# First matrices of a chain of per-sample layers: transfers and matmul operands addressed from registers in place of indirect gathers and one-hot picks

## The chip, the cores and the metric

One core of a Trainium2 chip runs the kernel. The metric is the device time of one execution in microseconds, as the median of several runs. The core has TensorE (PE, matmuls), VectorE (DVE), ScalarE (ACT), GpSimd (POOL) and SyncE (SP, which only issues transfers). SBUF and PSUM have 128 partitions; PSUM has eight banks of 128 x 512 fp32.

## The reference, cut

```python
# x (64, 64, 512) fp32; subject (64,) in 1..198, adapter (64,) in 0..7; C = 64 channels
x = x + einsum('bct,bcd->bdt', x, L0[subject])              # L0: 200 matrices 64 x 64
x = x + einsum('bct,bcd->bdt', x, L1[adapter])              # L1: 8 matrices
x = x + einsum('bct,bcd->bdt', x, L2[adapter]) + bias[adapter][:, :, None]
# then a gated MLP over the last axis, 512 -> 2048 -> 512, each matrix with a
# rank-16 correction chosen by adapter:
gate = x @ Wg + (x @ Ag[adapter]) @ Bg[adapter];  up = likewise with Wu, Au, Bu
h = silu(gate) * up
x = x + h @ Wd + (h @ Ad[adapter]) @ Bd[adapter]
```

With identities added, the first three layers of a sample are one 64 x 64 matrix, (I + L0[subject]) (I + L1[adapter]) (I + L2[adapter]), and a bias.

## The kernel before, in words

The 64 samples stand as 32 pairs (two samples of 64 channels fill 128 partitions), and the pairs are worked in four quarters of eight, each quarter in two halves t of four (TP = 4). For each quarter the MLP runs over 16 hidden blocks, called units; products are fp32 split in a high and a low fp32r part, and a Strassen-like scheme turns eight products of halves into seven. The matrices for quarters 1 to 3 are made while the units of the quarter before run. The opening, the code before the loop over units, makes those of quarter 0, with nothing to run beside. The change touches this opening alone. All order is written by hand: each engine has its own program and waits on semaphores.

The opening before, by engine:

- **SyncE** loads the subjects (`ints`), L2 (`w2_four`) and L1 (`w1_four`), waits for both, loads the first half of x (`load_x(0, 0)`), then after six picks the first weights (`load_weights(0)`), after the first gathers the second half of x, then b rows (`load_b(0)`); it stores `es_four` in `e_table`, waits for all four `w_done`, loads the weights of unit 1 and `bd_rows`, and goes on to `store_ad`, `store_b`.
- **VectorE** makes the row numbers of the gathers (`gather_numbers`), adds the identity to L2 (`e2_four`), compares the adapters of the quarter's samples with 0 to 7 (`eq_first`), adds to the product of L1 and I + L2 what makes it (I + L1)(I + L2) and keeps it in `es_four`, with zeros on both sides. It then makes for each of the eight pairs a one-hot pick matrix (`picks`, line 1334), widens what was picked (`picked`, 1342), and adds after the combining (`o_combine`, 1387). Numbers for later gathers follow (`block_rows`, `row_numbers`, `block_numbers`), `tables`, the low parts of the turned tokens (1454), `selectors` (1404), and from 1465 on the sums of tokens and their low parts (`o_low`, 1395), then `select` (1572, 1576).
- **GpSimd** issues eight indirect gathers of L0 rows (`ea_four`, line 766), then that of `ad_rows` (`gather_ad(0, 0)`), the low part of the b rows (`b_low(0)`, 803) and the gathers of `b_got`.
- **ScalarE** loads the adapters and the bias, makes the high parts of the first weights (`wg_hi`), adds the bias to each layer's result (974), copies the turned tokens (943), and between the halves makes the high part of the b rows (`b_high(0)`).
- **TensorE** runs 14 warm-up matmuls of 128 x 128 x 128 (`WARM_UP`, 1758), L1 times I + L2 (1913), the bias by pair (1917), 4 more warm-ups, the picks (1925: four matmuls of 64 columns a pair, one for each two adapters), the combining with the gathered L0 rows (1934: one matmul of 128 columns a pair), the layers (1943: one of 512 columns a pair) and the turns (transposes, 1762: four a pair), half 0 ahead of half 1, with only the combining of half 1 put before the turns of half 0. Then `first_product` begins at once with line 1735.

Each fp32 matmul stands in the trace as two passes, so that 16 picks' matmuls are 32 entries.

## Time and profile before

| | us |
|---|---|
| median of 3 runs | 1239.54 |
| lowest and highest of them | 1239.38, 1240.88 |
| the profiled execution, its own time | 1237.63 |
| its span, first to last instruction | 1235.8 |
| TensorE busy in the span | 1227.7 |
| first big product begins (line 1735) | 28.78 |

Times in the rows are counted from the span's start. A group in a timeline is a run of like instructions on one engine: its start, the time from its first start to its last end, and in brackets how long the engine had been idle before and what released it. A pass's duration overlaps its neighbours', so that the spacing of starts is the rate. A row such as "SPq" or "ACTq" is the issue of a transfer, and "to landing" is from the issue to the last byte.

### The profile page before, as it was taken

How to read it: one execution, taken by the hardware profiler on the slowest of the kernel's cores; microseconds unless marked ns; L12 is line 12 of the kernel's file. 1: busy time of each engine (PE TensorE's matmuls, PEld its weight loads, DVE VectorE, ACT ScalarE, POOL GpSimd, SP SyncE). 2: the span in 40 equal slices, each digit the busy share in tenths (PEclk: the TensorE clock that was granted, in tenths of full speed). 3: DMA queues.
4: the chain of work that ended last, by engine and by line, in shares of the span. 5: the costliest groups of instructions: out<-in, count | busy, mean ns of one | idle time of the engine just before them, and what ended most of it. 6: DMA issues, size and time to landing. Idle time of an engine off the chain costs nothing.

```text
span 1235.8 us, 18085 instructions
## 1 busy us (share of the span) xinstructions
PE 1227.7 (99%) x6190; PEld 1029.7 (83%) x6190; DVE 957.1 (77%) x1540; ACT 558.1 (45%) x1003; POOL 710.7 (58%) x598
## 2 busy tenths in 40 slices
PE   9999999999999999999999999999999999999998
PEld 8888888888888888888888888888888888888886
DVE  7887777887688777788678778777868877677775
ACT  4744445444544344454344444444534443444333
POOL 4676655558736556546864556555675554444453
PEclk9999999999999999999999999999999999999999
DMA  6866455556865455557496544546659442322323
GB/s 213 295 214 220 126 153 186 162 163 185 289 223 162 124 158 144 164 162 213 142 332 191 178 128 143 166 137 187 198 180 314 160 120 80 93 84 86 113 89 107
DMA packets 141690, 209.60 MB, mean 170 GB/s; under 512 B 44192, under 2 KB 88480, under 8 KB 141600
## 3 DMA queue, kind: packets, MB, share of 16 engines
q1 hardware_dynamic: 117696, 135.45, 34.8%
q0 software_dynamic: 23040, 71.85, 19.0%
q8 instruction: 51, 0.84, 0.3%
q10 hardware_dynamic: 864, 1.15, 0.3%
q14 instruction: 39, 0.32, 0.1%
HBM read 164.36 MB, written 44.04 MB: 169 GB/s over the span
## 4 chain that ended last, share of the span: by engine, by line
PE 97%; DVE 2%; issue 0%; ACT 0%; POOL 0%; DVEq 0%; POOLq 0%
PE px L1735 29%; PE pd L1735 28%; PE py L1735 14%; PE pz L1735 7%; PE pz L1752 3%; PE pv L1781 2%; PE pv L1779 2%; PE pd L2074 2%; PE py L1752 2%; PE px L1752 2%; PE pd L1762 1%; PE px L1886 1%; PE py L1886 1%; PE pd L1871 1%; PE px L1758 1%; PE pd L1904 0%
## 5 line engine op out<-in xcount | busy, mean ns | idle before, releaser
L803 POOL TENSOR_TENSOR h_lo<-g,h_hi 128x512 fp32r<-128x512 f32 x127 | 182.4, 1437 | 298.0 <-ACT h_hi L943 297.2
L766 POOL DMA_INDIRECT b_got<-b_table,idx_b x192 | 198.5, 1034 | 59.9 <-issue 49.9
L1735 PE MATMUL px<-xo_hi,wg_hi 128*128 128x512 f32 x516 | 207.2, 402 | 1.3 <-DVE wg_lo L1382 0.9
L1513 DVE TENSOR_TENSOR acc<-pd,acc 128x512 f32<-128x512 f32 x248 | 164.3, 684 | 51.6 <-PE pd L1735 51.6
L1382 DVE TENSOR_TENSOR wg_lo<-w_raw,wg_hi 128x512 fp32r<-128x512 f32 (+1 forms) x256 | 182.8, 720 | 26.5 <-ACT wg_hi L943 26.4
L1735 PE MATMUL px<-xo_hi,wg_lo 128*128 128x512 f32 x516 | 202.5, 392 | 0.0
L1735 PE MATMUL px<-xo_lo,wg_hi 128*128 128x512 f32 x516 | 201.0, 389 | 0.0
L943 ACT ACTIVATE wg_hi<-w_raw 128x512 fp32r<-128x512 f32 (+1 forms) x260 | 146.0, 570 | 121.1 <-PE py L1752 74.6
L1735 PE MATMUL pd<-wd_hi,h_hi 128*128 128x512 f32 x504 | 199.7, 396 | 0.0
L1735 PE MATMUL pd<-wd_lo,h_hi 128*128 128x512 f32 x504 | 197.9, 393 | 0.0
L1735 PE MATMUL pd<-wd_hi,h_lo 128*128 128x512 f32 x504 | 196.6, 390 | 0.0
L943 ACT ACTIVATE h_hi<-g 128x512 fp32r<-128x512 f32 x128 | 80.9, 632 | 195.0 <-DVE g L1607 76.1
L1735 PEld LDWEIGHTS px<-xo_hi,wg_lo 128*128 128x128 f32 x516 | 96.8, 188 | 22.1
L1735 PEld LDWEIGHTS px<-xo_hi,wg_hi 128*128 128x128 f32 x516 | 96.9, 188 | 19.1 <-issue 2.3
L1735 PEld LDWEIGHTS pd<-wd_hi,h_lo 128*128 128x128 f32 x504 | 94.6, 188 | 21.8
L1735 PE MATMUL py<-xo_hi,wg_hi 128*128 128x512 f32 x260 | 111.6, 429 | 0.0
L1735 PEld LDWEIGHTS px<-xo_lo,wg_hi 128*128 128x128 f32 x516 | 97.5, 189 | 15.6
L1735 PEld LDWEIGHTS pd<-wd_hi,h_hi 128*128 128x128 f32 x504 | 94.6, 188 | 13.9
L1735 PEld LDWEIGHTS pd<-wd_lo,h_hi 128*128 128x128 f32 x504 | 94.8, 188 | 12.8
L1617 DVE TENSOR_TENSOR g<-g,up 128x512 f32<-128x512 f32 x64 | 100.4, 1569 | 3.6 <-ACT g L1181 2.7
L943 ACT ACTIVATE g<-px 128x512 f32<-128x512 f32 x64 | 38.2, 598 | 141.2 <-PE px L1735 141.2
L1735 PE MATMUL py<-xo_hi,wg_lo 128*128 128x512 f32 x260 | 101.8, 391 | 0.0
(331 smaller groups left out, 2439.6 us busy)
## 6 DMA issues: line engine op xcount, KB each, us to landing
w_raw<-w_gu SPq DMA_DIRECT2D x65, 512.0 KB, 4.8
wd_raw<-w_dn SPq DMA_DIRECT2D x64, 256.0 KB, 3.5
xo_hi<-xops SPq DMA_DIRECT2D x21, 512.0 KB, 6.0
xo_lo<-xops SPq DMA_DIRECT2D x21, 512.0 KB, 7.3
acc<-x SPq DMA_DIRECT2D x8, 1024.0 KB, 6.8
ad_raw<-ad_table SPq DMA_DIRECT2D x16, 512.0 KB, 4.3
ad_table<-ad_rows_kept SPq DMA_DIRECT2D x12, 512.0 KB, 6.5
xops<-st_hi SPq DMA_DIRECT2D x24, 256.0 KB, 2.8
```

The source lines that it names most:

```text
L766: gp.indirect_dma_start(out=dst, out_offset=None, in_=rows_of, in_offset=bass.IndirectOffsetOnAxis(ap=rows.bitcast(U32), axis=0)).then_inc ...
L803: return gp.tensor_tensor(dst, src_raw, src_hi, ALU.subtract)
L943: return act.activation(dst, src, ACT.Copy)
L1382: dve.tensor_tensor(wg_lo[:, lo:hi, :], weights_of(n, g), wg_hi[:, lo:hi, :], ALU.subtract).then_inc(w_done[g], 1)
L1513: ins = dve.tensor_tensor(dst, pd[j][:, :], dst, ALU.add)
L1617: dve.tensor_tensor(g1[:, :], g1[:, :], up1[:, :], ALU.mult).then_inc(h_done[1], 1)
L1735: ins = pe.matmul(psum, w_parts[wi], x_parts[xi], start=(start and i == 0), stop=(stop and i == 2), skip_group_check=more)
L1752: ins = pe.matmul(psum[:, tokens], b_got[:, CHUNKS * t + c, first:first + P], u[:, m, t, cols], start=(start and c == 0), stop=True, skip_ ...
L1779: pe.matmul(pv[:, tok], ad[:, half, 2 * t + a, :, :].rearrange("p g n -> p (g n)"), hs[0][:, tok], start=(half == 0 and a == 0), stop=True ...
L1781: ins = pe.matmul(pv[0:HC, tok], ad[:, half, 2 * t + a, 0, :], hs[1][:, tok], start=False, stop=True, skip_group_check=True)
L1886: ins = pe.matmul(ua_bank(q, t, 0)[:, a * HALF:(a + 1) * HALF], w_parts[wi][:, cols], (xo_hi, xo_lo)[xi][:, k, tok], start=(cp == c == a = ...
L2074: pe.matmul(pd[0][:, :], f_one[:, :], acc[:, (q + 1) % 2, PAIR_ORDER[i], :], start=True, stop=True).then_inc(layer_mm, 1)
```

## The change

- SyncE and ScalarE each read the 16 subjects of quarter 0 from DRAM into registers, and TensorE the 16 adapters (`first_values`). The row transfers of L0 are plain transfers of 64 rows for one sample, with the address from a register (`first_rows`): samples of half s = 0 on SyncE's queue, s = 1 on ScalarE's, four for each half t and queue, 16 in all.
- L1 and L2 are laid out by adapter on 64 partitions (`w1_all`, `w2_all`) and loaded on ScalarE's queue. Their product takes eight matmuls of 64 columns in place of four; `es` holds for each adapter zeros, the matrix, zeros.
- Picks, widening and the addition after the combining go. The identity is added to the L0 rows before (`first_sum`, VectorE, in place), and the combining is one matmul of 64 columns a sample whose right operand is `es_cols` at a column from a register. ScalarE copies the result out of PSUM (`f_four`), two pairs a copy.
- Warm-up matmuls 11 and 4, not 14 and 4. Layers and turns are interleaved on TensorE: layers 0, 1, 2, turn 0 of half 0, layer 3, turn 1 and so on; ScalarE's bias additions and copies follow that order.
- The high part of the first weights and of the first b rows move from ScalarE to GpSimd, where the eight gathers were.
- SyncE's waits in the opening go in part: weights of unit 0 and both halves of x are issued behind row transfers without one; the weights of unit 1 come before the store of `e_table`. VectorE makes index numbers, tables and selectors directly after the second sum of rows, and waits for the store of `e_table` before the first sums of tokens, since `es` now lies where S1 is written.

```diff
-WARM_UP = (14, 4)
+WARM_UP = (11, 4)
...
+        es_cols = flat(acc[0:C, 1, 2:5, :])
+        es = by_adapter(es_cols)
+        w1_all = by_adapter(up1[0:C, :])
+        w2_all = by_adapter(g0[0:C, :])
+        e2 = by_adapter(g1[0:C, :])
+        ea = [flat(acc[0:C, 1, i:i + 2, :]).rearrange("p (s n) -> p s n", s=2 * TP) for i in (0, 6)]
+        f_four = [four(up0[:, :]), four(vacc[:, 0, :])]
...
+        of_banks = ((pz, pd[2]), (px, pv))
+
+        def first_rows(engine, t, s, subjects):
+
+            of_half = w0_rows[s * SUBJECTS * C:(s + 1) * SUBJECTS * C].rearrange("(u c) n -> u c n", c=C)
+            for j in range(TP):
+                rows = of_half[bass.ds(subjects[2 * (TP * t + j) + s], 1)].rearrange("u c n -> (u c) n")
+                engine.dma_start(ea[t][:, 2 * j + s, :], rows).then_inc(oe_in[t], 16)
...
-            sp.wait_ge(ints_in, 2 * 16)
-            sp.wait_ge(e0_in, 2 * 16)
+            sp.dma_start(ints[:, 1, :], adapter.partition_broadcast(P)).then_inc(ints_in, 16)
+            subjects = first_values(mybir.EngineType.SP, subject, SUBJECTS)
+            first_rows(sp, 0, 0, subjects)
             load_x(0, 0)
-            sp.wait_ge(pick_made, TP + 2)
+            first_rows(sp, 1, 0, subjects)
             load_weights(0)
-            sp.wait_ge(oe_in[0], TP * 16)
             load_x(0, 1)
             sp.wait_ge(x_in[0][1], 16)
             load_b(0)
+            load_weights(1)
             sp.wait_ge(oe_add, 1)
...
-            gp.wait_ge(idx_done, 1)
-            for t in range(2):
-                for j in range(TP):
-                    gather_rows(ea_four[t][:, j, :], w0_rows, idx_first[:, TP * t + j:TP * t + j + 1], oe_in[t])
+            gp.wait_ge(raw_in[0], 16)
+            for g in range(4):
+                gp.tensor_copy(wg_hi[:, 2 * g, :], w_raw[:, 0, g, :]).then_inc(w_hi_done[g], 1)
             gp.wait_ge(idx_a_done, 1)
             gather_ad(0, 0)
+            gp.wait_ge(*piece_in(0))
+            gp.tensor_copy(part(st_hi[:, piece(0)[0], :]), st_lo[:, piece(0)[0], :]).then_inc(b_hi_done, 1)
             b_low(0)
...
-            act.dma_start(ints[:, 1, :], adapter.partition_broadcast(P)).then_inc(ints_in, 16)
+            act.dma_start(w2_all, w2_rows.rearrange("p (a n) -> p a n", a=ADAPTERS)).then_inc(e0_in, 16)
+            act.dma_start(w1_all, w1_cols.rearrange("p (a n) -> p a n", a=ADAPTERS)).then_inc(e0_in, 16)
+            subjects = first_values(mybir.EngineType.Activation, subject, SUBJECTS)
+            first_rows(act, 0, 1, subjects)
             act.dma_start(bias_src, bias_pairs).then_inc(bias_in, 16)
+            first_rows(act, 1, 1, subjects)
+            act.dma_start(ints[:, 0, :], subject.partition_broadcast(P)).then_inc(subjects_in, 16)
...
+            for t in range(2):
+                for i in range(2):
+                    act.wait_ge(of_mm, 2 * t + i + 1)
+                    copy(f_four[t][:, 2 * i:2 * i + 2, :], four(of_banks[t][i][:, :])[:, 0:2, :]).then_inc(of_kept, 1)
...
+            for p in range(3):
+                o_bias(p)
+            for j in range(TP):
+                o_a1_high(j)
+                o_bias(j + 3)
+            o_bias(QP - 1)
+            for j in range(TP):
+                act.wait_ge(o_turn, TP + j + 1)
+                copy(acc[:, 1, :, j * P:(j + 1) * P].rearrange("p (k c) n -> p k c n", c=2)[:, 0:4:3],
+                     turn_banks[j][:, :].rearrange("p (k c n) -> p k c n", k=2, c=2)).then_inc(o_a2_kept, 1)
...
+            def first_sum(t):
+
+                dve.wait_ge(oe_in[t], 2 * TP * 16)
+                own_part = ea[t].rearrange("p (j s) (h n) -> p j (s h) n", s=2, h=2)[:, :, 0:4:3, :]
+                dve.tensor_tensor(own_part, own_part, ident[0:C, 0:C].unsqueeze(1).unsqueeze(1).to_broadcast([C, TP, 2, C]),
+                                  ALU.add).then_inc(ea_done, 1)
...
+            first_sum(0)
             dve.wait_ge(e2_done, 1)
             dve.wait_ge(oe_mm, 1)
-            dve.tensor_tensor(es_four[:, :, C:2 * C], four(pv[:, 0:TP * C]), e2_four, ALU.add).then_inc(oe_add, 1)
+            dve.tensor_tensor(es[:, :, C:2 * C], by_adapter(pv[0:C, :]), e2, ALU.add).then_inc(oe_add, 1)
+            first_sum(1)
+            row_numbers()
+            block_numbers()
+            tables()
+            gather_numbers()
+            selectors(0, 0)
...
             sums(1)
+            dve.wait_ge(e_out, 2 * 16)
...
+            adapters = first_values(mybir.EngineType.PE, adapter, ADAPTERS)
             pe.wait_ge(consts, 5)
             warm_up(WARM_UP[0])
             pe.wait_ge(e0_in, 2 * 16)
             pe.wait_ge(e2_done, 1)
-            for j in range(TP):
-                ins = pe.matmul(pv[:, j * C:(j + 1) * C], w1_four[:, j, :], e2_four[:, j, :], start=True, stop=True)
+            for i in range(ADAPTERS):
+                ins = pe.matmul(pv[0:C, i * C:(i + 1) * C], w1_all[:, i, :], e2[:, i, :], start=True, stop=True)
             ins.then_inc(oe_mm, 1)
...
             def o_combine(t):
-                pe.wait_ge(oe_in[t], TP * 16)
-                pe.wait_ge(eb_done, t + 1)
+                pe.wait_ge(ea_done, t + 1)
                 for j in range(TP):
+                    for s in range(2):
+                        first = j % 2 * P + s * C
+                        column = adapters[2 * (TP * t + j) + s] * (3 * C) + C
+                        ins = pe.matmul(of_banks[t][j // 2][:, first:first + C], ea[t][:, 2 * j + s, :],
+                                        es_cols[:, bass.ds(column, C)], start=True, stop=True)
+                    if j % 2:
+                        ins.then_inc(of_mm, 1)
...
-            picked(range(TP + 2))
             o_combine(0)
-            picked(range(TP + 2, QP))
-            o_layers(0)
+            o_combine(1)
             pe.wait_ge(bias_done, 1)
-            o_combine(1)
+            o_layer(0)
+            o_layer(1)
             for j in range(TP):
-                pe.wait_ge(o_layer_a, j + 1)
-                turn(0, 0, j, pd[j]).then_inc(o_turn, 1)
-            o_layers(1)
+                o_layer(j + 2)
+                o_turned(0, j)
+            o_layer(6)
+            o_turned(1, 0)
+            o_layer(7)
+            for j in range(1, TP):
+                o_turned(1, j)
```

## Rows read from the trace of the kernel before

**Rows 1.** The page: span, busy time by engine, chain by engine.
```profile
span 1235.8 us, 18085 instructions
PE 1227.7 (99%) x6190; PEld 1029.7 (83%) x6190; DVE 957.1 (77%) x1540; ACT 558.1 (45%) x1003; POOL 710.7 (58%) x598
...
PE 97%; DVE 2%; issue 0%; ACT 0%; POOL 0%; DVEq 0%; POOLq 0%
```

**Rows 2.** TensorE's waits after the warm-up, whole span: waiting line, releaser, us in total, times, longest.
```profile
PE px L1735 <- DVE wg_lo L1382: 0.9, 1, 0.9
PE px L1735 <- DVE up L1560: 0.4, 1, 0.4
```

**Rows 3.** Timeline of TensorE, opening: start, length, engine, line, operation, tiles, count.
```profile
1.94 5.78 PE L1758 MATMUL px<-ident 128*128 128x128 f32 x28 [1.94 <-POOL ident L810]
7.55 1.00 PE L1913 MATMUL pv<-acc 128*128 128x64 f32 x8
...
8.59 1.14 PE L1758 MATMUL px<-ident 128*128 128x128 f32 x8
9.56 1.90 PE L1925 MATMUL pz<-vacc,g 128*128 128x64 f32 x16
...
14.87 1.11 PE L1934 MATMUL pv<-acc 128*128 128x128 f32 x8
...
17.55 3.65 PE L1943 MATMUL pd<-acc 128*128 128x512 f32 x8
...
28.78 0.48 PE L1735 MATMUL px<-xo_hi,wg_hi 128*128 128x512 f32 x1
...
48.00 0.48 PE L1752 MATMUL pz<-u,b_got 128*128 128x192 f32 x3
```

**Rows 4.** Timeline of VectorE, opening.
```profile
16.09 0.69 DVE L1387 TENSOR_TENSOR acc<-pv,acc 128x512 f32<-128x512 f32 x1 [0.85 <-PE pv L1934]
...
18.64 0.14 DVE L1262 TENSOR_SCALAR f_one<-f_one 128x1 int32<-128x1 int32 x1
18.70 0.16 DVE L1263 TENSOR_SCALAR f_one<-ea_one 128x16 int32<-128x16 int32 x1
...
30.23 1.29 DVE L1465 TENSOR_TENSOR acc<-acc 128x512 f32<-128x512 f32 x2
...
47.04 0.54 DVE L1576 TENSOR_TENSOR u<-pd,u_mask 128x384 fp32r<-128x384 f32 x1
```

**Rows 5.** Timeline of ScalarE, opening: the first issue, a copy of turned tokens.
```profile
0.75 0.41 ACTq L977 DMA_DIRECT2D eb_one<-adapter  x1
...
28.85 0.61 ACT L943 ACTIVATE acc<-pv 128x512 f32<-128x512 f32 x1
```

**Rows 6.** Timeline of GpSimd, opening: one of eight gathers, b_low, a gather of b_got.
```profile
16.41 0.94 POOL L766 DMA_INDIRECT acc<-w_rows,st_lo  x1 [0.30 <-issue]
...
25.65 2.38 POOL L803 TENSOR_TENSOR st_lo<-st_lo,st_hi 128x1024 fp32r<-128x1024 f32 x1 [2.04 <-ACT st_hi L943]
...
40.11 1.24 POOL L766 DMA_INDIRECT b_got<-b_table,idx_b  x1 [0.16 <-issue]
```

**Rows 7.** Timeline of SyncE's queue, opening: the halves of x.
```profile
6.66 0.38 SPq L570 DMA_DIRECT2D acc<-x  x1
...
14.59 0.38 SPq L570 DMA_DIRECT2D acc<-x  x1
```

**Rows 8.** Transfers issued up to 45 us: kind, count, KB each, median us to landing.
```profile
acc<-x SPq DMA_DIRECT2D x2, 1024.0 KB, 5.3
...
acc<-w_pairs SPq DMA_DIRECT2D x1, 256.0 KB, 4.9
...
acc<-w_rows,st_lo POOLq DMA_INDIRECT x8, 3.7
b_got<-b_table,idx_b POOLq DMA_INDIRECT x5, 5.6
...
eb_one<-subject SPq DMA_DIRECT2D x1, 32.0 KB, 3.7
```

173 lines of the change are left out of this document (46 added, 127 removed).

## The prediction

> **What bounds the kernel now.** I read the page first: TensorE is busy 1227.7 us of a span of 1235.8 us, and the chain of work that ended last is TensorE for 97% [rows 1]. The list of TensorE's waits over the whole span has, after the 1.94 us before the first warm-up matmul [rows 3], one entry of 0.9 us and one of 0.4 us [rows 2]. So TensorE's stream is packed from 1.94 us on, and a change to the opening is worth exactly the time by which it brings forward the first big product (called T below, 28.78 us now), if nothing behind it becomes late. The timeline of TensorE says what fills the time to T [rows 3]: 28 warm-up passes from 1.94, the eight passes that multiply L1 with L2 at 7.55, eight more warm-up passes, and then from 9.56 to 17.55 the one-hot picks (64 passes of 64 columns in five rows, of which one stands) and the first combining (8 passes, 14.87). From 17.55 to T run layers, combining for the second half and turns. (Each fp32 matmul is two passes.)
>
> The other engines are close behind. VectorE works without a gap from the weight parts near 16.7 to 48 us; its first token sums start at 30.23, 1.45 after T, and its selection ends at 47.58 [rows 4], where TensorE's product with b_got, which needs it, starts at 48.00 [rows 3]: 0.4 us of slack. Whoever brings T forward must bring this VectorE chain forward by as much.
>
> **Removed on TensorE.** 9.56 to 17.55 is 7.99 us; less about 1.0 for the combining in it, the picks are 7.0 us, 0.11 us a pass [rows 3]. All go. VectorE loses eight picks, two widenings and two additions, all of the shape that takes 0.69, some 8 us [rows 4]; the eight indirect gathers leave GpSimd.
>
> **Added on TensorE.** The combining is now one matmul a sample: 16 matmuls, 32 passes of 64 columns. At the picks' rate that is 32 x 0.11 = 3.5 us, against 2 x 0.95 for the old 2 x 8 passes: +1.6. The L1-L2 product has 16 passes instead of 8, with stationary operands half as wide; between no change and 8 x 0.11 = 0.9. I take 0.5, and it lies where TensorE otherwise warms. Three warm-up matmuls fewer free 6 x 0.2 = 1.2 us there. Layers and turns are the same instructions in another order: 28.78 - 17.55 less 0.9 for the second combining (8 passes like those at 14.87) = 10.3 us [rows 3]. If only TensorE's work counted, T would move by 7.0 - 1.6 = 5.4 us, and by some tenths more for the warm-ups. But now operands decide, so I follow those.
>
> **Reading registers.** SyncE, ScalarE and TensorE each read 16 integers from DRAM into registers first. No row shows such a read. The nearest rows are one issue of a transfer, 0.41 [rows 5], and the landing of the smallest one, the 32 KB of subjects, 3.7 [rows 8]. I take 1.1 us, near the low end, because 64 bytes move and no transfer is built; the ends stay for the range. On TensorE it lies beside the 1.94 us that it waits for the identity [rows 3], so up to 1.2 us of it costs nothing.
>
> The Trainium skill, page "Runtime: NRT & Kernel Launch", section "Instruction fetch mechanics", puts a register load at about 200 ns a register even in bulk. By that estimate 16 registers are 3.2 us, the row addresses are known 2.1 us later, and the gain below shrinks to 2.6 us. No run here shows it yet.
>
> **Row transfers with addresses from registers.** An issue is 0.38 to 0.41 us [rows 5, 7]. To it come some two or three register operations; the nearest row is the step between two tiny independent VectorE instructions, 0.06 us (18.64 to 18.70) [rows 4], so 0.5 to 0.6 in all; I take 0.6, and for the range 0.4 to 1.0. ScalarE issues the L2 and L1 matrices (0.9), reads (1.1), issues 4 rows (2.4), the bias (0.4) and 4 rows (2.4): from 0.75 it ends at 8.0. SyncE issues the adapters (0.4), reads, 4 rows, x's first half (0.4), 4 rows: it ends at 7.45, with x's first half issued at 5.0, where it was 6.66 [rows 7]. A transfer of this size lands 3.7 after its issue as an indirect gather, with 0.94 us of GpSimd's own work in it [rows 6, 8]; behind a megabyte of x I take 3.3. The first eight rows are then there at 4.55 + 3.3 = about 8.0, the second eight at 7.4 + 3.3 = 10.7.
>
> **The chain to T.** L1, issued second at 1.2, lands in 4.9 [rows 8], at 6.1; 0.68 of VectorE for the sum with the identity gives 6.8, TensorE's product 8.2. First sum of rows, 0.69 [rows 4], ends at 8.7, the addition into es at 9.4. The bias lands near 5.6 + 4.0 = 9.6, and TensorE waits for it ahead of four warm-ups (1.0) [rows 3]: 10.7 at worst, and the eight matmuls of the first combining (1.8) run to about 12.0 with some overlap of my allowances. The second needs the second rows: 10.7 + 0.69 = 11.4. So rows and TensorE meet near 11.7, the second combining ends at 13.5, and layers and turns run on to 23.8. TensorE's reading of its operand address from a register costs between nothing (its sequencer is ahead of the array) and 16 x 3 x 0.06 = 2.9 us; nearest is nothing, since the picks also ran at 0.11 a pass and a matmul here fills the array for 0.22; I take 0. The new order has ScalarE copy the first turn of the second half after all eight bias additions, so T waits for that copy: 0.61 [rows 5], of which half lies beside the last turn: +0.3. T = 24.1, gain 28.8 - 24.1 = 4.7 us.
>
> **Does the rest follow?** VectorE: the second half of the first sums could start when the fourth copy is done, T + 0.9, and end at T + 1.6, where it ended at 31.52 = T + 2.7 [rows 4]; its slack grows by 1.1. Ahead of that it has, from 11.4 on, the numbers for indices, tables and selectors (6 us), weight parts (1.4), and low parts of the first turns as they come: done before T. The e_table store, which VectorE now awaits before the sums, is issued some 8 us ahead of them and lands like x within 5.3 us [rows 8]; cover 2.7 us, and if gone it delays VectorE by what is missing. GpSimd takes two jobs from ScalarE: the four weight copies (bounded by 1.2 and, as its subtraction, 2.38 for 1024 columns) and the first b copy (same bounds) [rows 6]. Queued behind them are gather_ad, b_low and the b_got gathers. The indices come at about 13, not 22, and the weights by 12.5, so even at 2.4 + 2.4 this queue is still some 4 us earlier than now; the gather at 40.11 lands 5.6 later [rows 6, 8], 2.3 before the product at 48.00 needs it [rows 3], and its predecessor, the b copy on ScalarE, moves with T. The second half of x is issued near 8.8 rather than 14.59 and lands within 5.3 [rows 8], before layer 4 at 17.9. What is late next is VectorE again, no worse than now. I count nothing for it.
>
> **Sum.** The profiled execution took 1237.63 us, its span 1235.8 [rows 1] and 1.8 around it; 1237.6 - 4.7 = 1232.9. The median of the runs shown lies 1.9 above it, 1239.54, so 1239.54 - 4.7 = 1234.8.
>
> **Rivals.**
> A, register work is dear: reading costs 3.3 us, near the 3.7 of a small landing [rows 8], not 1.1, or TensorE's operand addresses cost their 2.9. Either moves T to 26.3 to 27.0, gain 1.8 to 2.5: 1237.4. For it: no row excludes it. Against: the gap in TensorE's work while it waits for rows hides half of the second.
> B, the other sign: the registers are read one after another with a round trip each. Beyond 1.1 + 4.7 = 5.8 us for 16, or 0.36 each, T is later than now. At 0.5 us each it is 8.0: T = 31.0, 2.2 us slower, 1241.8. For it: a small transfer's round trip is 3.7 us [rows 8]. Against: one read of a few words has no transfer's descriptors.
> C, TensorE's clock. The profile grants 1.00 (2.4 GHz) in its clock row throughout, yet the first 28 passes take 0.21 us each and the later eight 0.14 at most [rows 3], so some slowness stands at the start. New holes, ahead of the rows, could bring it back for a few us: at double length for 3 us of work T moves by 3, 1237.9. The Trainium skill, page "TensorE: Matmul & The Clock Gate", section "HAM oscillation — how this bites in real kernels", says that holes in the stream return TensorE to 1.2 GHz; that would be this case. My holes are 1 to 2 us, with work between.
> D, something later is late: the gain at T is given back in units 1 to 3, by b_got or VectorE. Time 1239.5. Against: the slacks above.
> E, rows land in 2.3 us rather than 3.3 and issues cost 0.45, so that the second rows are there by 8.4 and TensorE's own stream decides: 6.8 + 1.4 (product) + 0.2 (bias) + 1.0 (warm-ups) + 3.5 + 10.3 = 23.2, or 22.7 if the product takes 0.9. Gain 5.6 to 6.1: 1233.4 to 1233.9. Nothing in these rows allows more. Against: the bias too would have to land by 8.
>
> **How the numbers follow.** Forecast 0.55 (1234.0 to 1236.0 by itself), A 0.15, B 0.06, C 0.06, D 0.06, E 0.12. A measurement of this kernel can tell about 0.2%, 2.5 us. Faster by more: forecast, E, a third of A and C: 0.55 + 0.12 + 0.07 = 0.74, and a little of the forecast's neighbours, 0.76. Slower by more: half of B and a little for unnamed causes, 0.06. Same 0.18. The range reaches over E, with half a microsecond for the spread of the runs, and most of A and C: 1232.9 to 1238.0.
>
> **What would show it.** Right: TensorE's first big product near 24.1; L1758's second group followed by 32 passes in 3.5 us or with one gap of 1 to 2 us in it, released by VectorE's sum of rows; layers and turns in 10.3 to 10.6 us; TensorE's waits after T unchanged at about 1.3 us. A: the first row transfers on SyncE issue later than 2.5 us, or the 32 passes are spaced by more than 0.11. B: they issue after 7. C: layer passes longer than 0.65 us. D: new entries in the list of TensorE's waits after T. The prediction is wrong if T moves and the time does not, or if T moves by less than 3 us.

## The result and the profile after

| | before | after |
|---|---|---|
| median, us | 1239.57 | 1245.18 |
| lowest, highest of 5 runs | 1239.38, 1240.88 | 1245.07, 1245.43 |
| profiled execution, own time | 1237.63 | 1245.23 |
| its span | 1235.8 | 1243.3 |
| first big product begins (T) | 28.78 | 35.63 |
| span less T | 1207.0 | 1207.7 |

The change makes the kernel slower by 5.6 us: ratio 1.0043, interval 1.0032 to 1.0054. The forecast was 1234.8, at most 1238.0. The last row of the table says where to look. Behind T the two executions are the same within 0.7 us, so the loss lies in the opening. The profiled execution of before took 1.7 us less than the lowest of its five runs, so the two profiles differ by 7.6 us where the medians differ by 5.6; what follows splits T of the profiles. Two later executions, one of x7_interleave and one of x11_best, took about 1735 us at a mean clock of 0.65, and the medians below count them while the ratios leave them out.

The page of after, span, busy time, and shares of the chain by engine, against rows 1:

```profile
span 1243.3 us, 18046 instructions
PE 1229.8 (99%) x6144; PEld 1029.0 (83%) x6144; DVE 950.9 (76%) x1523; ACT 557.5 (45%) x1002; POOL 705.2 (57%) x595
...
PE 96%; DVE 2%; issue 1%; ACTq 0%; DMA 0%; ACT 0%; DVEq 0%
```

TensorE runs 46 passes fewer than before and is nevertheless busy 2.1 us longer. Some of its passes must have become slower. Its waits in after, whole span (waiting line, releaser, us in total, times, longest), against rows 2:

```profile
PE px L1743 <- issue: 4.7, 1, 4.7
PE py L1903 <- DMA vacc<-bias_pairs: 2.1, 1, 2.1
PE px L1720 <- DVE wg_lo L1379: 0.9, 1, 0.9
PE px L1720 <- DVE up L1545: 0.7, 1, 0.7
PE px L1720 <- ACT up L944: 0.3, 1, 0.3
```

Two are new: the start at 4.7 instead of 1.94, and 2.1 us for the bias. The last three, behind T, sum to 1.9 us, where before had 1.3. The timeline of TensorE in after shows the order, against rows 3:

```profile
4.69 5.04 PE L1743 MATMUL px<-ident 128*128 128x128 f32 x22 [4.69 <-issue]
9.65 1.69 PE L1899 MATMUL pv<-g,up 64*64 64x64 f32 x16
13.43 0.41 PE L1903 MATMUL py<-st_lo,vacc 128*128 128x32 f32 x2 [2.09 <-DMA vacc<-bias_pairs]
...
15.09 1.97 PE L1913 MATMUL pz<-acc 64*128 x8
...
22.11 5.49 PE L1922 MATMUL pd<-acc,up 128*128 128x512 f32 x6
...
35.63 0.47 PE L1720 MATMUL px<-xo_hi,wg_hi 128*128 128x512 f32 x1
```

The 32 combining passes (line 1913) run from 15.09 to 22.1: 7.0 us, 0.22 a pass, where the picks took 0.11. The first three layers (line 1922, six passes) take 5.49, or 0.91 a pass; half of that is what a pass took before (3.65 for eight). From 28.1 on the passes have their old length. So from 14 to 28 us TensorE ran at half speed, and the windows of after say so too (window, its length, PE's busy time and passes, granted clock, DMA share, GB/s):

```profile
12.00:14.00 2.00, 0.57 (x5) 1.00 1.20 283
14.00:16.00 2.00, 2.00 (x12) 0.58 0.84 265
...
26.00:28.00 2.00, 2.00 (x6) 0.51 1.16 394
28.00:32.00 4.00, 4.00 (x21) 1.00 0.92 351
```

The granted clock is 1.00 (2.4 GHz) until past 14, then 0.50 (1.2 GHz), and 1.00 again from 28. What TensorE did before the fall: it stood idle from 11.3 to 13.4, waiting for the bias.

Why the bias was late is in the queues. First SyncE, then ScalarE in after (start of the first issue, length of the group, count), against rows 7 and 5:

```profile
0.75 0.39 SPq L643 DMA_DIRECT2D eb_one<-adapter  x1
4.31 2.70 SPq L231 DMA_DIRECT2D acc<-w_rows  x4
7.06 0.58 SPq L578 DMA_DIRECT2D acc<-x  x1
```

```profile
4.90 2.47 ACTq L231 DMA_DIRECT2D acc<-w_rows  x4
7.41 0.60 ACTq L982 DMA_DIRECT2D vacc<-bias_pairs  x1
```

SyncE's register reads stand between 1.14 and 4.31: 3.2 us. The loads themselves (duration in ns three times, start in us):

```profile
L235 SPq TENSOR_LOAD <-subject_ptr x1: 867/867/867, 1.2 to 1.2; - x1
...
L235 PEldq TENSOR_LOAD <-adapter x1: 2816/2816/2816, 1.8 to 1.8; - x1
...
L235 SPq TENSOR_LOAD <-subject x1: 2027/2027/2027, 2.1 to 2.1; - x1
L235 ACTq TENSOR_LOAD <-subject x1: 1765/1765/1765, 3.0 to 3.0; - x1
```

Each engine first loads a pointer, in 0.87 to 0.93 us, and then the 16 values, in 1.77 us on ScalarE, 2.03 on SyncE and 2.82 on TensorE. The bias is issued at 7.41, 0.35 behind a megabyte of x. The landings in after (count, KB each, median us to landing), first of the issues from 4 to 7.8 us, then of those from 7.8 to 11 us, against rows 8:

```profile
acc<-w_rows SPq DMA_DIRECT2D x4, 32.0 KB, 2.1
acc<-w_rows ACTq DMA_DIRECT2D x4, 32.0 KB, 2.0
vacc<-bias_pairs ACTq DMA_DIRECT2D x1, 64.0 KB, 6.0
```

```profile
acc<-w_rows SPq DMA_DIRECT2D x4, 32.0 KB, 5.4
acc<-w_rows ACTq DMA_DIRECT2D x4, 32.0 KB, 5.4
```

The bias takes 6.0 us and arrives at 13.4. A row lands in 2.0 to 2.1 us ahead of x and in 5.4 behind it. The first sum of rows on VectorE starts at 9.33. The second:

```profile
15.44 0.68 DVE L1341 TENSOR_TENSOR acc<-acc,ident 64x512 f32<-64x512 f32 x1 [3.30 <-DMA acc<-w_rows]
```

It ends at 16.1, when combining of the first half is under way, and is needed at 18.5. It stops nobody here; with the bias on time it is next, as x5_x_behind shows below.

### The profile page after: what moved, and what is told of

It is laid out like the page before. It is cut to its first block, busy times and chain, and to the rows that moved or that the text cites. A ratio compares the mean times of both kernels' runs of the same rounds, so it can differ in the third digit from the quotient of the medians.

```text
span 1243.3 us, 18046 instructions
## 1 busy us (share of the span) xinstructions
PE 1229.8 (99%) x6144; PEld 1029.0 (83%) x6144; DVE 950.9 (76%) x1523; ACT 557.5 (45%) x1002; POOL 705.2 (57%) x595
## 4 chain that ended last, share of the span: by engine, by line
PE 96%; DVE 2%; issue 1%; ACTq 0%; DMA 0%; ACT 0%; DVEq 0%
PE px L1720 28%; PE pd L1720 27%; PE py L1720 14%; PE pz L1720 7%; PE pz L1737 3%; PE pv L1766 2%; PE pv L1764 2%; PE pd L2055 2%; PE py L1737 2%; PE px L1737 2%; PE pd L1747 1%; PE py L1871 1%; PE px L1871 1%; PE pd L1856 1%; PE pd L1922 1%
## 5 line engine op out<-in xcount | busy, mean ns | idle before, releaser
L1379 DVE TENSOR_TENSOR wg_lo<-w_raw,wg_hi 128x512 fp32r<-128x512 f32 (+1 forms) x256 | 183.3, 722 | 27.0 <-issue 16.1
L1720 PEld LDWEIGHTS px<-xo_hi,wg_lo 128*128 128x128 f32 x516 | 96.8, 188 | 22.1
L1720 PEld LDWEIGHTS pd<-wd_lo,h_hi 128*128 128x128 f32 x504 | 94.8, 188 | 12.9
```

The lines of the kernel that those rows point to most:

```text
L1379: dve.tensor_tensor(wg_lo[:, lo:hi, :], weights_of(n, g), wg_hi[:, lo:hi, :], ALU.subtract).then_inc(w_done[g], 1)
L1720: ins = pe.matmul(psum, w_parts[wi], x_parts[xi], start=(start and i == 0), stop=(stop and i == 2), skip_group_check=more)
```

## The experiments

Two theories stood at the start. K, clock: the idle time before the bias cost TensorE its clock, and that is most of the loss. R, registers: reading them is dear and delays everything. A third, that operand addresses from registers slow the passes, would be seen as slow passes at full clock. "T", "span less T" and "low" are of one profiled execution, "time" is the median, with the kernel before run beside each group on the same chip (1238.2, 1238.4, 1239.8 and 1240.1 us in the four groups), so the ratios are what can be compared across groups. "Low" is the stretch in which the clock row of the profiled execution stands at 0.50, read from windows of half a microsecond. The profiled execution is not always near the median: in x1_fill, x3_bias_first and x12_x_first it is 1.4 to 2.6 us below it, in x14_both 2.0 and in x13_fill_more 8.6 above.

| run | T | span less T | time | ratio (interval) | low |
|---|---|---|---|---|---|
| x1_fill | 29.11 | 1207.3 | 1239.98 | 1.0017 (1.0005 to 1.0028) | none |
| x2_const | 32.88 | 1207.1 | 1242.51 | 1.0030 (1.0021 to 1.0040) | 10.6 to 24.2 |
| x3_bias_first | 32.56 | 1207.2 | 1243.07 | 1.0033 (1.0019 to 1.0048) | 16.7 to 23.5 |
| x4_late_read | 36.18 | 1207.1 | 1245.42 | 1.0055 (1.0039 to 1.0072) | 10.7 to 27.7 |
| x5_x_behind | 32.71 | 1207.3 | 1242.47 | 1.0032 (1.0019 to 1.0044) | 17.0 to 23.8 |
| x6_all | 34.14 | 1207.4 | 1244.09 | 1.0050 (1.0033 to 1.0067) | 11.5 to 25.1 |
| x7_interleave | 30.67 | 1208.3 | 1240.67 | 1.0023 (1.0012 to 1.0035) | none |
| x8_half_read | 37.76 | 1207.0 | 1246.90 | 1.0071 (1.0054 to 1.0088) | 12.9 to 30.0 |
| x9_const_fill | 29.20 | 1207.6 | 1239.31 | 0.9994 (0.9982 to 1.0007) | 17.7 to 21.1 |
| x10_few_warm | 35.90 | 1207.2 | 1246.08 | 1.0052 (1.0035 to 1.0069) | see text |
| x11_best | 33.51 | 1207.3 | 1241.97 | 1.0016 (1.0006 to 1.0026) | 17.7 to 24.6 |
| x12_x_first | 28.63 | 1207.2 | 1240.29 | 1.0006 (0.9993 to 1.0018) | 9.5 to 12.9 |
| x13_fill_more | 40.74 | 1207.4 | 1241.31 | 1.0015 (1.0002 to 1.0027) | 14.5 to 31.6 |
| x14_both | 33.80 | 1207.5 | 1241.10 | 1.0009 (0.9999 to 1.0018) | 8.6 to 15.4 |

In after it is 14.4 to 28.0.

### Filling the hole

```diff
+            warm_up(9)
             pe.wait_ge(bias_in, 16)
             pe.wait_ge(eq_done, 1)
```

> The changed kernel with nine more warm-up matmuls ahead of TensorE's wait for the bias, which fill the hole from 11.3 to 13.4 us in its trace. Theory K (the hole costs the clock; the granted clock is 0.50 from 14.3 to 27.6 us and in that stretch the 32 combining passes take 7.0 us instead of 3.5 and three layers 5.3 instead of 2.6): the clock stays at 1.00, the first big product comes near 29.5 instead of 35.6, and the time is 1239.2. Theory R (late operands alone make the kernel slow, the clock is only a sign): the time stays at 1245 within 0.5.

Only warm-up passes are added, ahead of the wait that stood idle. The timeline of TensorE in this run:

```profile
10.78 2.27 PE L1743 MATMUL px<-ident 128*128 128x128 f32 x18
13.44 0.41 PE L1904 MATMUL py<-st_lo,vacc 128*128 128x32 f32 x2 [0.39 <-DMA vacc<-bias_pairs]
...
14.75 1.10 PE L1914 MATMUL pz<-acc 64*128 x8
```

The bias product starts at 13.44, as in after (13.43), and all that differs is behind it: the combining passes run at 0.11, the first three layers take 2.84 instead of 5.49, and T is 29.11 instead of 35.63. So the hole cost 6.5 us in the profiled execution, and 18 useless passes give it back. The median gains less, from 1.0043 to 1.0017 of the kernel before, some 3 us. K holds. It also ends the third theory: eight combining passes take 0.94 us from one group's start to the next here, and 0.94 with fixed addresses in x9_const_fill.

The ten executions differ more than those of after, from 1238.21 at a mean clock of 1.000 to 1243.54 at 0.996. By the mean clock, some of them still lose it for a time; more on this below.

### Fewer warm-ups in the kernel before

Fewer warm-ups in the kernel before, and nothing else. Its picks and combining must become slow too if K is not about the new code.

```diff
-WARM_UP = (14, 4)
+WARM_UP = (5, 0)
```

> The kernel before with 5 and 0 warm-up matmuls in place of 14 and 4, nothing else: TensorE then idles from about 4 to 7.2 us and again ahead of the picks. Theory K (a hole in the opening costs the clock over what follows, in any kernel): granted clock 0.50 for several us after 8, picks and combining near 0.21 us a pass, first big product 5 us or more later than 28.78, time 1243 or more. Rival (the clock fall belongs to the changed kernel's narrow matmuls): first big product as before, time within 0.5.

TensorE's timeline in this run:

```profile
7.41 1.94 PE L1913 MATMUL pv<-acc 128*128 128x64 f32 x8 [2.97 <-DVE acc L1423]
...
9.93 3.67 PE L1925 MATMUL pz<-vacc,g 128*128 128x64 f32 x16 [0.21 <-DVE vacc L1433]
```

and one of its windows:

```profile
12.00:16.00 4.00, 4.00 (x21) 1.00 0.52 159
```

The real work starts where it did (7.41, before 7.55), but the picks take 0.22 us a pass, not 0.11, and T is 7.1 us later: 1.0052. So the warm-ups of the kernel before are worth 6 to 7 us. This is not quite the case of after, though: the ten warm-up passes start 0.21 us apart, as the first ones do in every run, and no group of passes before 23.6 us runs faster. The full rate was never reached ahead of the hole, so the run prices a late rise, not a fall. And the clock's row reads 1.00 while passes take twice their time: it shows a later fall, not a clock that has not yet risen. The first warm-up passes of the kernels here, at about 0.2 us each for a product that later takes 0.12 to 0.13 (x1_fill, 2.27 for 18), are slow under a 1.00 too. The length of a pass is the surer witness.

### Reading registers, and the places of the transfers

Subjects and adapters fixed in the code, so that no register is read (left out: that they come from the input):

```diff
-            subjects = first_values(mybir.EngineType.SP, subject, SUBJECTS)
+            subjects = FIXED_SUBJECTS
...
-            adapters = first_values(mybir.EngineType.PE, adapter, ADAPTERS)
+            adapters = FIXED_ADAPTERS
```

> The changed kernel with 16 subjects and adapters of the first quarter fixed in the program, so that nothing is read into registers and no address comes from one; the selection by the inputs is left out for that quarter. Theory R (register reads of 3 us on three engines and 0.13 us at each of 16 row transfers are the whole lateness): rows and bias land 3 to 4 us earlier, TensorE has no hole over 1 us, the clock stays, first big product near 25, time 1234.5. Rival Q (the row and bias transfers are late because a megabyte of x shares the queues): rows of the second half still land 5 us after their issue, first big product at 28 or later, time 1238 or more.

Its bias issue on ScalarE, and TensorE's bias product:

```profile
1.97 2.65 ACTq L233 DMA_DIRECT2D acc<-w_rows  x4
4.66 0.60 ACTq L984 DMA_DIRECT2D vacc<-bias_pairs  x1
```

```profile
10.84 0.64 PE L1905 MATMUL py<-st_lo,vacc 128*128 128x32 f32 x2 [2.68 <-DMA vacc<-bias_pairs]
```

The bias is issued 2.75 us earlier and its product starts 2.59 earlier, T moves by 2.75 (35.63 to 32.88), and the hole is still there, 2.68 us long, because TensorE starts earlier too; the clock falls as before. R is real, 2.8 us of it, and on its own it does not bring the gain. The four row transfers take 2.65 us to issue with constant addresses and 2.47 with addresses from registers, one about every 0.65 us in both. The chain of after shows 0.05 and 0.03 us of register arithmetic ahead of each, and an issue of 0.48 to 0.51; with constants the issue itself is 0.62. So addresses from registers cost nothing here, though the arithmetic is there.

The bias ahead of ScalarE's register read:

```diff
+            act.dma_start(bias_src, bias_pairs).then_inc(bias_in, 16)
             subjects = first_values(mybir.EngineType.Activation, subject, SUBJECTS)
             first_rows(act, 0, 1, subjects)
-            act.dma_start(bias_src, bias_pairs).then_inc(bias_in, 16)
```

> The changed kernel with the bias transfer put ahead of ScalarE's register read; nothing else. The bias is there by 7, so TensorE's hole of 2.1 us goes and the first combining starts near 12.5 instead of 15.1. Then the second sum of rows (ends at 16.1) decides: first big product near 28.5, time 1238, if the clock holds over the new hole of some 1.7 us between the combinings. If the clock falls in that hole (theory K in its strict form, any hole of 2 us is enough), it is near 32 and the time 1241.5.

The bias product comes at 10.86 without a wait. The hole moves on, to 12.2 to 14.9: combining waits 2.70 us for the addition into es, which stands on VectorE behind the first row sum, and that one's last row, on ScalarE's queue, now goes out behind x (7.33). T is 32.56: 3.1 us better than after. Nearly all of it is the shorter time at the low clock, 6.8 us for 13.7, since combining starts only 0.15 earlier.

TensorE's read behind its warm-ups, so that these start at 1.94 again:

```diff
-            adapters = first_values(mybir.EngineType.PE, adapter, ADAPTERS)
             pe.wait_ge(consts, 5)
             warm_up(WARM_UP[0])
+            adapters = first_values(mybir.EngineType.PE, adapter, ADAPTERS)
```

> The changed kernel with TensorE's register read behind its first eleven warm-up matmuls instead of ahead of them. The warm-up starts at 1.94 instead of 4.69. If TensorE's own read is what costs (rival P), everything on TensorE comes 2.7 us earlier: time 1242.5. If the bias and rows decide (my theory), the product of L1 and L2 comes earlier and the hole ahead of the bias grows to 5 us, the combining starts at 15.1 as before, and the time is 1245 within 0.7.

What looks like an improvement makes the hole longer, 5.77 us, as nothing but the bias decided; the clock is low from 10.7, not 14.4, and T is 0.5 later, by as much as the bias product (13.97 for 13.43). So TensorE's start at 4.7 in after cost nothing.

The first half of x behind all row transfers of SyncE:

```diff
             first_rows(sp, 0, 0, subjects)
+            first_rows(sp, 1, 0, subjects)
             load_x(0, 0)
-            first_rows(sp, 1, 0, subjects)
```

> The changed kernel with SyncE's issue of x's first half put behind both groups of its row transfers instead of between them. Theory Q (the bias and the second rows are late because the megabyte of x, issued 0.35 us ahead of the bias, is being moved: bias 6.0 us to land against 3.3 in the run where it was issued early): the bias lands by 11.2 instead of 13.4, the second sum of rows starts by 14 instead of 15.4, TensorE has no hole above 1 us ahead of the bias, the clock holds, first big product near 27.5, time 6 us below the changed kernel. Rival (the landing is slow for a reason of the small transfers themselves): both land as late as before and the time moves by less than 1 us.

The landings in this run, and TensorE:

```profile
acc<-w_rows ACTq DMA_DIRECT2D x8, 32.0 KB, 2.0
...
vacc<-bias_pairs ACTq DMA_DIRECT2D x1, 64.0 KB, 2.0
```

```profile
16.86 1.89 PE L1913 MATMUL px<-acc 64*128 x8 [2.55 <-DVE acc L1341]
```

With x out of the way the bias lands in 2.0 us, not 6.0, and a row in 2.0, not the 5.4 of the second rows in after. That is the price of x beside small transfers. But now the last rows of ScalarE meet x; the second sum comes at 16.0, and the hole of 2.55 us stands between the halves of the combining, with the same effect on the clock: one hole was exchanged for another, T = 32.71.

All at once (x and bias issued ahead of the reads, each queue reading only its own eight subjects, TensorE's read late, WARM_UP = (14, 4)):

```diff
+            load_x(0, 0)
             subjects = first_values(mybir.EngineType.SP, subject, SUBJECTS)
             first_rows(sp, 0, 0, subjects)
-            load_x(0, 0)
```

> A version built from what the runs showed: each of SyncE and ScalarE reads only its own 8 subjects, x's first half and the bias are issued ahead of these reads, TensorE reads behind its warm-up matmuls, of which there are again 14. The read of 2.7 us should halve; row transfers of 0.65 us each then end at 8.9 on SyncE and 9.5 on ScalarE, with x already landed. Second sum of rows near 12.8, first big product near 26, time 2.5 to 3 us below the kernel before. If the clock falls in the hole of about 1 us between the two combinings: 2 us or more above it. If transfers of rows land as late as behind x (5 us): first big product near 27.5.

This time the hole, 2.61 us, stands ahead of the L1-L2 product: L1, issued 0.15 us behind x's first half, lands in 8.5 us where it took 3.6 in after, and the product starts at 10.85. SyncE's queue in this run, where the issue of x ends at 1.63:

```profile
8.05 5.22 SPq L231 DMA_DIRECT2D acc<-w_rows  x8
```

Half the registers take twice the time, 1.63 to 8.05, 6.4 us. Two things were changed in the read, so the halved read was run by itself, beside no x:

```diff
-                values.unsqueeze(0)[:, 0:2 * QP], [engine],
+                values.rearrange("(q s) -> s q", s=2)[first:first + 1, 0:QP], [engine],
```

> The changed kernel with SyncE and ScalarE reading only the 8 subjects that each uses (every second one), nothing else. If a read costs by the register (2.7 to 3.2 us for 16, 0.17 to 0.2 each): reads take 1.4 to 1.6, first rows, bias and second rows are issued 1.4 earlier. The bias then lands near 12, the hole ahead of it shrinks to 0.7, the clock holds in most runs, first big product near 27.7, time 1.5 us below the changed kernel with the low clock and up to 7 below without. If a read costs as a whole (contiguous words fetched together), 8 words in steps of two cost as much as 16 and nothing moves.

SyncE's load of the values and its first row transfers in this run:

```profile
L237 SPq TENSOR_LOAD <-subject x1: 3371/3371/3371, 2.1 to 2.1; - x1
```

```profile
5.64 2.61 SPq L231 DMA_DIRECT2D acc<-w_rows  x4
```

Eight values, every second word, load in 3.37 us, 0.42 each; sixteen contiguous ones took 2.03, 0.13 each. With the pointer and what stands between, the read takes 4.5 us (1.14 to 5.64) for 3.2. So it is the stride that is dear, 1.3 us here, and reading beside x adds another 1.9. I had not expected either. The hole is 4.18 us and T 37.76, the latest but one in the table.

### The interleaving by itself

The kernel before, with only the new order of layers and turns and the b copy on GpSimd. To interleave, its second combining had to go ahead of layers 2 and 3 of the first half.

```diff
-            o_layers(0)
             pe.wait_ge(bias_done, 1)
+            o_layer(0)
+            o_layer(1)
             o_combine(1)
             for j in range(TP):
...
+                o_layer(j + 2)
+                o_turned(0, j)
...
```

> The kernel before with only the interleaving of layers and turns (on TensorE and ScalarE) and, so that ScalarE can follow it, the high part of the first b rows on GpSimd. My reading: the interleaving moves nothing, since TensorE was packed there; the first big product comes 0 to 0.3 us later than at 28.78, the time is that of the kernel before within 0.5. Rival (the interleaving itself makes TensorE wait for ScalarE's bias additions): 1 us or more slower.

T is 1.9 us later. 1.25 of it is a wait for the second half's gathered rows, which the old order had hidden; without it this stretch takes 11.75 us (17.67 to 30.67), where before has 11.23. The order itself brings nothing. Of what it cost in after, 10.65 us for layers and turns against 10.3, the prediction had 0.3. The clock stayed at 1.00 over this wait of 1.25 us, which stands between passes of 512 and of 128 columns.

### Looking for a better opening

Fixed values and 12 warm-up matmuls ahead of the bias wait (left out: as in x2_const):

```diff
+            warm_up(12)
             pe.wait_ge(bias_in, 16)
```

> Fixed subjects and adapters for the first quarter (the selection by inputs left out there), as in the earlier run, and twelve more warm-up matmuls in the hole of 2.7 us ahead of the bias, so that the clock is held. Against the filled version with register reads (first big product at 29.1) this leaves the price of reads and register addresses alone. Theory: bias by 10.8, combining from 12.1, second sum by 13.8, first big product near 26.2, time 2.5 us below the kernel before. Rival (with the clock held, reads are hidden by the transfers of x anyway): first big product at 28.5 or later, time as the filled version.

TensorE's timeline in this run and its windows:

```profile
15.88 1.05 PE L1916 MATMUL pv<-acc 64*128 64x64 f32 x8
16.86 4.54 PE L1925 MATMUL pd<-acc,up 128*128 128x512 f32 x6
```

```profile
16.00:18.00 2.00, 2.00 (x12) 0.93 0.17 30
18.00:20.00 2.00, 2.00 (x4) 0.50 0.85 250
```

Without register reads and without a hole over 0.35 us, the clock still fell, at 17.7, behind the 32 passes of 64 columns, and came back at 21.1. The one execution of ten at a mean clock of 1.000 took 1236.05, 3.7 below the median of the kernel before and 2.1 below its fastest; the median, 1239.31, is no different from it. Every profile of the changed opening with a hole of 2 us or more lost the clock, then, but it was also lost without one.

The order that the runs so far spoke for (TensorE's read late, bias first, adapter sum ahead of the row sum, x behind the rows, WARM_UP = (11, 11) and 6 warm-ups between the combinings):

```diff
             first_rows(sp, 0, 0, subjects)
-            load_x(0, 0)
             first_rows(sp, 1, 0, subjects)
+            load_x(0, 0)
...
             o_combine(0)
+            warm_up(6, px)
             o_combine(1)
```

> A version from the runs so far: contiguous reads kept (16 words, 3 us; every second word took 4.5), bias ahead of ScalarE's read, TensorE's read behind its first warm-ups, x behind all row transfers on SyncE, es added ahead of the first sum of rows, and warm-up matmuls (11, 11, 6 more between the combinings) over all holes. First rows there at 10.2, first combining from 11; the second rows are the open point: if ScalarE's last row lands behind x as in the run with x behind (16.0), first big product near 28.3 and the time equal to the kernel before within 0.7; if it lands by 13.5, 26.3 and 2.4 us below. The clock should hold in nearly all runs (theory K); if it falls all the same, 1241 or more.

Combining starts at 11.13, 4 us ahead of after, and then stands 3.01 us for the second rows: ScalarE issues its last until 10.9, x goes out at 9.3. That asked for x ahead of all rows, with the second half of x and the weights only behind them (3 warm-ups between the combinings instead of 6, all else as in x11_best):

```diff
+            load_x(0, 0)
             first_rows(sp, 0, 0, subjects)
-            load_x(0, 0)
             first_rows(sp, 1, 0, subjects)
+            sp.wait_ge(oe_in[1], 2 * TP * 16)
+            load_x(0, 1)
             load_weights(0)
-            load_x(0, 1)
```

> The changed kernel, with nothing left out of the work, put in another order: ScalarE issues the bias before it reads its registers; TensorE reads its registers behind its first warm-up; SyncE issues the first half of x ahead of its row transfers, and the second half and the weights only once the second rows have landed; the adapter sum stands ahead of the first row sum; the warm-up is (11, 11), with 3 passes more between the two halves of the combining products. The price looked for: the 2.5 to 3.0 us of waiting for the second row sum in the two runs before, which the theory puts down to rows that queue behind the first half of x after it is issued at 9.3. By the theory x is nearly through when the last rows are issued, the second sum is ready at 13.0 to 13.7 instead of 16.0 to 16.8, no hole before the second combining is over 1 us, the clock stays at 1.00, T is 25.5 to 27.5 and the time 3 to 1 us below the kernel before. The rival: rows are late whatever moves beside them (each is issued 0.65 us behind the last, and all land late while x moves), the second sum is at 15 or later, the clock falls again, T is 30 or more and the time above the kernel before.

VectorE's second sum and TensorE in this run:

```profile
13.47 0.68 DVE L1342 TENSOR_TENSOR acc<-acc,ident 64x512 f32<-64x512 f32 x1 [1.03 <-DMA acc<-w_rows]
```

```profile
13.28 1.10 PE L1914 MATMUL pz<-acc 64*128 x8
...
16.07 1.10 PE L1914 MATMUL px<-acc 64*128 x8
```

The sum starts at 13.5 and is there at 14.15, a little behind the 13.0 to 13.7 expected, and no hole stands between the combinings. But the clock fell all the same, from 9.5 to 12.9, after a gap of 1.1 us at 6.6 while TensorE read its registers. TensorE's load of the 16 values, first in x11_best, then in this run:

```profile
L235 PEldq TENSOR_LOAD <-adapter x1: 1822/1822/1822, 4.0 to 4.0; - x1
```

```profile
L235 PEldq TENSOR_LOAD <-adapter x1: 3598/3598/3598, 4.0 to 4.0; - x1
```

It starts at the same place in both, but here x is issued at 4.23, beside it, and in x11_best at 9.3. So the gap that most likely cost the clock is itself a price of x first: the read did not end under the warm-ups. This time it hit the 22 warm-up passes, 4.33 us where x11 has 2.70 for as many, so that combining began at 13.28. T is 28.63 in the profiled execution, the fastest of the ten (1237.65), and the median is that of the kernel before: 1.0006, interval 0.9993 to 1.0018. It has the lowest ratio of the complete variants, and no gain. My own sum for T was also low by the layers and turns: 18.0 where combining ends, and 10.65 to T.

Do the narrow passes lose the clock by themselves? The filled kernel with two warm-up matmuls more after every four combining products (16 passes more in all, twice what the expectation counted), and the same added to x12 with 4 ahead of the bias wait:

```diff
                     if j % 2:
                         ins.then_inc(of_mm, 1)
+                        warm_up(2, pd[3])
```

> The changed kernel with 9 warm-up passes ahead of TensorE's wait for the bias (as in the first experiment) and 2 more after every 8 combining products. It asks whether those narrow products (64 columns each) can themselves cost the clock where no hole stands before them. If only a hole costs the clock, the 8 passes more cost 8 x 0.11 = 0.9 us on the path: T is 29.1 + 0.9 = 30.0, the time 0.9 us above the first experiment's, and its runs scatter as before. If the narrow products cost it in some executions, these passes hold it: the runs scatter less, and the median is no higher than the first experiment's against the same kernel before (ratio 1.0017).

> The order of the run with x first, with 2 warm-up passes more after every 8 combining products and 4 ahead of the wait for the bias: 12 passes, 1.3 us at 0.11 each if all of them stand on the path. If x first alone holds the clock, this run is up to 1.3 us slower than it. If it does not because TensorE still stands idle for 1 to 2 us before the second combining, this run is the faster: T 26 to 28, and the time 0 to 2 us below the kernel before. If the second rows are late as in the rival of that run, the fillers cannot cover 2.5 us and both lose.

In x13, eight of ten executions lie between 1240.68 and 1242.07 at a mean clock of 0.999 or 1.000, where x1_fill had five of ten at 0.998 or less. The other two took 1247.6 and 1249.9, and the profiled one is the later:

```profile
14.41 0.55 PE L1904 MATMUL py<-st_lo,vacc 128*128 128x32 f32 x2 [2.29 <-DMA vacc<-bias_pairs]
```

In it the bias came 1 us later than in x1, the warm-ups did not reach that far, and the clock was low from 14.5 to 31.6. (Its T in the table is that execution's; by the times, the median's lies some 9 us earlier, an estimate.) Eight of ten against five of ten, on two chips, speaks for the wider passes holding the clock where no hole stands; it does not show it. Fillers of a fixed number do not hold it against a transfer that is late. x14 has 12 matmuls, 24 passes, more than x12 and is no better; its profiled execution lost the clock from 8.6 to 15.4, behind a gap of 1.8 us, again under TensorE's read.

## Why the prediction was wrong

**What bounds the kernel.** Held. A change to the opening is worth the move of T: span less T is 1207.0 before, 1207.7 after, and between 1207.0 and 1207.6 in all twelve variants of the changed opening, with T from 28.6 to 40.7. Of the two variants of the kernel before, x10_few_warm has 1207.2 and x7_interleave 1208.3, 0.6 of it in new waits behind T.

**T.** This failed: 24.1 forecast, 35.63 measured, 11.5 us. The runs split it.

- *Clock, 6.5 us* (after less x1_fill). It was rival C, with a chance of 0.06 and a size of 3 us "for 3 us of work". Both were wrong. This is the step that failed: the sum put the clock at nothing, and had no row for how long it stays away once it is lost; it stayed for 13.7 us of packed work, all of the combining and three layers. And I called the holes "1 to 2 us, with work between" without asking what the warm-ups of the kernel before are for. The row that TensorE's passes start at 0.21 was read, and not carried through the new order, where I took three warm-ups out of the sum as freed time. By the Trainium skill, page "TensorE: Matmul & The Clock Gate", section "HAM oscillation — how this bites in real kernels", a hole returns TensorE to 1.2 GHz; the trace agrees (0.50 from 14.4 to 28.0, behind a hole of 2.1 us).
- *The bias, 3.8 us*: forecast to land at 9.6, it was needed and late at 13.4. The forecast added 4.0 to the end of its issue; counted from the start, as the trace does, the issue was forecast at 5.15 and came at 7.41, 2.3 later, of which 1.8 is the read of the subjects (2.9 us between ScalarE's issues, not 1.1). The other 1.5 is the landing, 6.0 and not 4.5, behind x. Rival A covers the read, at about its size of 2.2; no rival had the landing.
- *The rest, 1.2 us*: 0.2 for the bias product and warm-ups (13.44 to 14.75, for 1.1), 0.2 for the combining (3.7, for 3.5), 0.1 for layers and turns, and 0.7 for what I had struck off as an overlap of allowances, which wasn't there: 10.7 + 3.5 is 14.2, and I wrote 13.5.

6.5 + 3.8 + 1.2 = 11.5.

**Reading registers.** Mis-sized by 1.8 us on ScalarE and 2.1 on SyncE. The Trainium skill, page "Runtime: NRT & Kernel Launch", section "Instruction fetch mechanics", gives about 200 ns a register, by estimate 3.2 us for 16. SyncE's whole read takes 3.2, but the trace splits it otherwise: 0.87 for the pointer, and 0.13 a value (0.11 on ScalarE, 0.18 on TensorE). I had weighed this estimate and taken the low end of a range from rows that showed something else. For eight strided words the load takes 0.42 each. TensorE's read moved its start by 2.75 us (4.69 for 1.94) instead of hiding behind the identity, and that cost nothing, since the bias decided (x4_late_read).

**Row transfers.** 0.60 an issue forecast, 0.61 to 0.68 measured: right, though not for the reason given, as constant addresses cost the same (x2_const). The landing was not: 3.3 forecast, 2.0 to 2.1 measured for the first rows and 5.4 for the second, behind x. The first sum starts at 9.3 (8.0 forecast), the second at 15.4 (10.7 forecast). These 4.7 us cost nothing in after, since with the bias late the second combining had its turn only at 18.6 (and at 16.6 in x1_fill, where the sum ends at 16.0). They are what stood in the way in x5_x_behind and x11_best.

**Operand addresses and the combining.** No cost forecast, none found (0.11 to 0.12 a pass in x1_fill, the same in x9_const_fill with fixed addresses). Layers and turns forecast 10.6, measured 10.65 (18.46 to 29.11 in x1_fill).

**The picks.** 7.0 us forecast to go, and they went. But they also were the work that kept TensorE busy while rows came. Removing them laid bare the arrival of the transfers, and that is where the forecast gain went: even with the clock held, T is 29.11 against 28.78. The second half of the mistake is that TensorE's work (12.0) and the transfers (11.4) were said to "meet near 11.7", where the later of the two decides, and that both were taken at their optimistic end.

**Does the rest follow?** Held. The slack of VectorE grew a little, its last selection ended 18.3 us behind T, before 18.8. VectorE's selection in after:

```profile
53.37 0.55 DVE L1561 TENSOR_TENSOR u<-pd,u_mask 128x384 fp32r<-128x384 f32 x1
```

GpSimd in after, against rows 6, is 0.5 us earlier with b_low (25.18), though T is 6.9 later; I had put it 4 us earlier, and nobody waited for it.

**The range and the chances.** Rivals A and C were both partly true at once, and they add: a late bias makes the hole that costs the clock. I had priced them one by one. B, slower because reads cost over 0.36 us each, did not occur for the reads as written.

What stays open: how short a gap, among narrow passes, is enough to lose the clock. It was lost after gaps of 1.1, 1.8 and 2.1 us and more, and once (x9_const_fill) with none over 0.35, and kept in the profile of x1_fill with 0.39 and in that of x7_interleave with 1.25. No run varied the gap alone. Also open is what brings the clock back. In ten of the twelve profiles that lost it, it came back 2.8 to 5.9 us behind the first layer pass (512 columns) and never during the combining (64 columns); in the other two, x12_x_first and x14_both, it came back in the warm-ups. Whether the kind of work decides this, no run tested.

## What to carry to other kernels

Before taking work off TensorE near the start of a kernel, ask what comes in its place. If it is a wait of 2 us, price it at the wait plus the low clock on all the work behind it until the clock returns (here 6.5 us), not at the wait. Small transfers that decide go out ahead of big ones, and a read of registers goes behind all small issues that don't need it, but not beside a megabyte in flight (1.8 us became 3.6). If T is only moved by filling holes with passes that do nothing, compare with the old work that filled them: here the one-hot picks were that filler, and removing them gained nothing even in the best order.

## What the runs showed of the hardware

- A lost clock stays lost for 3.4 us (x9_const_fill, x12_x_first), 6.8 (x3, x5, x11, x14), 13.7 (after, x2, x6) or 17.1 (x4, x8, x13). Where the work is packed it costs about half of that: 6.5 us in after, for 13.7. The kernel before with its warm-ups cut, where the full rate came late, lost 7.1.
- The row of the granted clock reads 1.00 while passes of 64 columns take 0.22 us instead of 0.11 (x10_few_warm, from 7 to 24 us). It shows a fall, not a clock that has not yet risen; the length of a pass shows both.
- A read of 16 contiguous words into registers is two loads: 0.87 to 0.93 us for a pointer, then 1.8 us on ScalarE, 2.0 on SyncE, 2.8 on TensorE (after). Between its neighbours it takes 2.9 us on ScalarE and 3.2 on SyncE. Eight words at a stride of two take 4.5 on SyncE (x8_half_read), and 6.4 beside a megabyte in flight (x6_all). TensorE's 16 values took 1.8 us (x11_best) and 3.6 beside x (x12_x_first).
- A 64 KB transfer lands in 2.0 us with no x in flight (x5_x_behind), and in 6.0 when it is issued 0.35 us behind a megabyte on another queue (after); a 32 KB one in 2.0 to 2.1 ahead of x and in 5.4 behind it, in one execution (after).
- A row transfer of 64 rows is issued every 0.61 to 0.68 us, with a constant address as with one from a register. The issue of the same load of x took 0.39 us ahead of the row transfers (x12_x_first) and 0.58 directly behind four of them (after).
